# The further rounds of layer one: one guarded block at the last body instead of one at the head of each body

## What is computed

```python
def layer0(h, src, dst, w, W, b):
    h = h @ W + b
    msgs = w[:, None] * h[src]
    agg = segment_sum(msgs, dst, N)
    deg = segment_sum(w, dst, N)
    return relu(agg / (deg[:, None] + 1e-6))

def layer1(h, e, W_msg, b_msg, W_upd, b_upd, eps, src, dst):
    m = gelu(concatenate([h[src], e], -1) @ W_msg + b_msg)
    h = (1 + eps) * h + segment_sum(m, dst, N)
    return gelu(h @ W_upd + b_upd)

h = relu(layernorm(x));  x = x + layer0(h, src, dst, edge_weight, ...)
h = relu(layernorm(x));  x = x + layer1(h, edge_attr, ...)
```

## Time and profile before

| | us |
|---|---|
| runs | 2934.1, 2928.56, 2933.87 |
| median | 2933.87 |
| profiled execution, its time | 2940.75 |
| its span | 2938.9 |

### The profile page before, as it was taken

How to read it: one execution, slowest core, us unless ns; L and a number is a source line. 1 busy time by engine, 2 the same in 40 slices (tenths; PEclk the granted TensorE clock), 3 DMA queues, 4 the chain that set the end, 5 groups by cost and what they waited for, 6 DMA issues and landing times.

```text
span 2938.9 us, 72786 instructions
## 1 busy us (share of the span) xinstructions
PE 2615.2 (89%) x22325; PEld 2440.5 (83%) x22326; DVE 2088.3 (71%) x4375; ACT 1617.3 (55%) x5144; POOL 1820.8 (62%) x1911
## 2 busy tenths in 40 slices
PE   1788877887888888788999999999999999999999
PEld 1678777777777777777999999999999999999998
DVE  8766667667667666766777777777777777777774
ACT  2555555455555555545556656556656565665653
POOL 3355555555555555552777777777777777777771
PEclk9999998888888888888999999999999999999997
DMA  6010111110111111111454444544444545444442
GB/s 125 16 20 19 21 21 20 22 22 20 21 22 20 21 22 21 20 21 44 109 124 119 121 121 118 121 118 121 117 120 118 123 115 123 119 119 120 118 120 45
DMA packets 473383, 216.56 MB, mean 74 GB/s; under 512 B 264997, under 2 KB 442025, under 8 KB 473077
## 3 DMA queue, kind: packets, MB, share of 16 engines
q1 hardware_dynamic: 412404, 151.55, 19.8%
q0 software_dynamic: 60672, 62.25, 11.5%
HBM read 208.14 MB, written 5.51 MB: 73 GB/s over the span
## 4 chain that ended last, share of the span: by engine, by line
PE 52%; DVE 0%; ACT 0%; issue 0%; DVEq 0%
PE ps L917 38%; PE ps L1115 7%; PE ps L989 4%; PE ps L1104 3%; PE ps L1062 1%; PE ps L1018 0%; DVE rows L1446 0%; DVE parts L1211 0%; DVE sel L1442 0%; DVE room L1635 0%; ACT h_sb L847 0%; DVE h_sb L1666 0%; DVE h_sb L1671 0%; ACT h_sb L865 0%; DVE tick L1483 0%
## 5 line engine op out<-in xcount | busy, mean ns | idle before, releaser
L628 POOL DMA_INDIRECT rows<-p_table,idx x1176 | 1110.0, 944 | 395.5 <-issue 350.0
L917 PE MATMUL ps<-parts,pick_all 128*128 128x448 f32 x5488 | 1167.0, 369 | 2.2 <-DVE parts L1211 2.2
L917 PEld LDWEIGHTS ps<-parts,pick_all 128*128 128x128 f32 x5488 | 1017.8, 188 | 83.5 <-issue 2.6
L628 POOL DMA_INDIRECT rows<-h_table,idx x720 | 694.2, 964 | 616.1 <-ACT room L759 422.5
L720 ACT COPY adj<-ps 128x500 f32<-128x500 f32 (+1 forms) x848 | 394.8, 518 | 308.2 <-PE ps L927 298.0
L927 PE MATMUL ps<-hot_c,hot_p 128*128 128x125 f32 (+1 forms) x2336 | 470.7, 304 | 63.9 <-issue 57.3
L927 PEld LDWEIGHTS ps<-hot_c,hot_p 128*128 128x128 f32 x2336 | 393.0, 212 | 80.5 <-issue 72.2
L1442 DVE TENSOR_TENSOR sel<-ps,mask 128x896 f32<-128x896 f32 x196 | 214.0, 1092 | 310.1 <-PE ps L917 302.0
L1425 DVE TENSOR_SCALAR pick_all<-src_all,node_f 128x1792 fp32r<-128x1792 int16 x196 | 406.6, 2075 | 28.6 <-issue 26.2
L989 PE MATMUL ps<-onehot,room 128*65 128x72 f32 (+1 forms) x3400 | 227.0, 237 | 193.7 <-DVE onehot L1373 98.2
L989 PEld LDWEIGHTS ps<-onehot,room 128*65 128x65 f32 (+1 forms) x3400 | 197.7, 144 | 228.2 <-issue 118.2
(11 more groups left out here) (180 smaller groups left out, 2592.4 us busy)
## 6 DMA issues: line engine op xcount, KB each, us to landing
src_all<-keys SPq DMA_DIRECT2D x196, 448.0 KB
ea<-in_edge_attr_dram SPq DMA_DIRECT2D x196, 256.0 KB
rows<-p_table,idx POOLq DMA_INDIRECT x1176
rows<-h_table,idx POOLq DMA_INDIRECT x720
x_sb<-in_x_dram SPq DMA_DIRECT2D x6, 224.0 KB, 4.0
h_table<-h_sb SPq DMA_DIRECT2D x6, 224.0 KB
p_table<-h_sb SPq DMA_DIRECT2D x6, 224.0 KB
out_dram<-h_sb SPq DMA_DIRECT2D x6, 224.0 KB
```

The costliest lines, as they stand in the source:

```text
L628: nc.gpsimd.indirect_dma_start(out=rows[:, s, j, 0:D], out_offset=None, in_=table[:, :], in_offset=bass.IndirectOffsetOnAxis(ap=idx[:, s, ...
L917: last = nc.tensor.matmul(to, hot[:, k, t * P:(t + 1) * P], parts[:, part, k, :, :].rearrange("p a d -> p (a d)"), start=(k == 0 and part ...
```

## The change

`further_rounds` leaves the head of every body. A new function `all_rounds` is called in its place, but only in the last body of layer one (`if not ahead`), on PE and on DVE. It is guarded by one flag, `row_any`, the greatest of the bodies' bits, which one more reduction on DVE makes in the preparation. Inside it loops over the zones and their bodies with the old block. PE's wait on `s_sumTc` now stands before these loops and waits for all bodies' sums; an increment of `s_passed` next to it is gone.

```diff
@@ -256,6 +256,7 @@
         row_r = sb("row_r", [1, 3, BODIES])
         row_g = sb("row_g", [1, NG])
         row_b = sb("row_b", [1, BODIES, 2], i32)
+        row_any = sb("row_any", [1, 1], i32)
         slow_at = sb("slow_at", [1, SLOTS, JA], i32)
         node_i = sb("node_i", [P, 1], i32)
         with nc.sbuf_tensor("src_raw", [P, 2, G], i32) as src_raw, nc.sbuf_tensor("dst_raw", [P, 2, G], i32) as dst_raw:
@@ -959,13 +960,11 @@
                                             ones_col[:, :], start=True, stop=True)
                 last.then_inc(s_sum, 1)
 
-            def further_rounds(z, b, more):
-
-                with pe.If((more & (1 << SLOTS)) > 0):
+            def further_rounds(z, b):
+
+                with pe.If((more_flags(b) & (1 << SLOTS)) > 0):
                     count = pe.value_load(row_b[0:1, bass.ds(b, 1), 0], min_val=1, max_val=N)
                     before = pe.value_load(row_b[0:1, bass.ds(b, 1), 1], min_val=0, max_val=N * BODIES)
-                    pe.wait_ge(s_sumTc, b + 2)
-                    pe.sem_inc(s_passed, 1)
                     with pe.Fori(0, count) as i:
                         k = (before + i) * (TILES + 1)
                         for t in range(z.tiles):
@@ -1022,9 +1021,18 @@
                 blocks_of(ZONES[0], 0, s)
             adjacency_sums(ZONES[0], 0)
 
+            def all_rounds():
+
+                with pe.If(pe.value_load(row_any[0:1, 0:1], min_val=0, max_val=1) > 0):
+                    pe.wait_ge(s_sumTc, BODIES + 1)
+                    for z in ZONES:
+                        with pe.Fori(z.first, z.end) as b:
+                            further_rounds(z, b)
+
             def first(b, here, ahead, further):
                 more = more_flags(b)
-                further_rounds(here, b, more)
+                if not ahead:
+                    all_rounds()
                 if ahead:
                     blocks_of(ahead, b + 1, 0)
                 sums_back(here, b)
@@ -1314,6 +1322,7 @@
             meta(nc.vector.scalar_tensor_tensor(out=bits[:, :, 0], in0=row_r[:, 2, :], scalar=float(2 ** SLOTS),
                                                 in1=bits[:, :, 0], op0=ALU.mult, op1=ALU.add))
             meta(nc.vector.tensor_copy(row_i[:, :, 3], row_f[:, 2, :]))
+            meta(nc.vector.tensor_reduce(row_any[:, :], row_r[:, 2, :], AX.X, ALU.max))
             dve.wait_ge(s_base_ps, 1)
             meta(nc.vector.tensor_copy(base_bc[:, :], psS[:, 0:NG]))
             dve.wait_ge(s_dwt, 2)
@@ -1482,9 +1491,16 @@
 
                 nc.vector.memset(tick[:, s:s + 1], 0.0).then_inc(s_done, 1)
 
-            def further_rounds(z, b, more):
-
-                with dve.If((more & (1 << SLOTS)) > 0):
+            def all_rounds():
+
+                with dve.If(dve.value_load(row_any[0:1, 0:1], min_val=0, max_val=1) > 0):
+                    for z in ZONES:
+                        with dve.Fori(z.first, z.end) as b:
+                            further_rounds(z, b)
+
+            def further_rounds(z, b):
+
+                with dve.If((more_flags(b) & (1 << SLOTS)) > 0):
                     count = dve.value_load(row_b[0:1, bass.ds(b, 1), 0], min_val=1, max_val=N)
                     before = dve.value_load(row_b[0:1, bass.ds(b, 1), 1], min_val=0, max_val=N * BODIES)
                     with dve.Fori(0, count) as i:
```

## The result

| | before | after |
|---|---|---|
| median of the runs, us | 2931.22 (4 runs) | 2822.93 (4 runs, 2820.88 to 2834.17) |
| profiled execution, us | 2940.75 | 2820.88 |
| its span, us | 2938.9 | 2819.1 |
| granted clock of the span | 0.947 | 0.965 |

The ratio is 0.9639, with a 95% interval of 0.961 to 0.9667: 108 us faster in the median. The forecast was 2835, in a range of 2780 to 2873.

What follows compares the result with a forecast made beforehand. VectorE's serial stream with its hole was taken to bound layer one. Gains of 56.1 + 35.6 + 8 - 1 = 99 us took the profiled 2940.75 to 2842, and 7 less for the median gave 2835; range 2780 to 2873.

Steps and rivals of the forecast that it cites:

- The hole: VectorE's idle time in issue before each layer-one loop body, 7.5 to 8.2 us in zone 1, 6.8 in zone 0; code fetch.
- case (d): Rival: the hole is a fixed price of loads, compares and semaphores; gain only 5 to 10 us, about 2926; chance 0.05.
- The split of jump and back edge: Of VectorE's 7.6 us idle at a loop head, the jump over the rounds is about 3, the back edge about 4.
- The ring: VectorE's tile builds, TensorE's last window, sums and next tile product, whose release VectorE awaits: 25.45 us a body in zone 1.
- Case (a): Rival: the back edge keeps its stall; zone 1 stays at 25.45, zone 0 costs 4 us more, 2839; 0.72 together with the sum.
- zone 0's loop: Period falls from 21.97 to 19.0 us, the same kind of ring giving 18.8; 35.6 us over 12 bodies.
- zone 1's loop: Period falls from 27.32 to the ring's 25.45 us; 56.1 us over 30 bodies.
- the rest: Body 48's jump and flag load, 0.5 us, and one more VectorE reduction in the prologue, 0.3; together about -1 us.
- The straight bodies: Bodies outside the loops and the entries (14, 15, 16, 47): 2 us saved each, 8 in all, ends 0 and 10.
- Body 48: Keeps one jump, over about 530 VectorE instructions, with a second load of a flag; costs 0.5 us.
- case (b): Rival: fewer or shorter gaps give TensorE its full clock in the adjacency sums; 50 us more gain, 2785; chance 0.16.
- Case (c): Rival: TensorE's clock falls for the whole of the sums and tiles, sums about 14 us; about 2995; chance 0.02.

Runs made afterwards that it cites:

- e1b_dve_back: The changed kernel with VectorE's rounds put back at the head of every body, TensorE's at the last body only; 2925.06 us, ratio 0.9992.
- e2b_pe_back: The changed kernel with TensorE's rounds put back at the head of every body, VectorE's at the last body only; 2843.41 us, ratio 0.9715.
- e4_skip_a: The changed kernel with never-run blocks at VectorE's body heads: 40 instructions in zone 0's loop, 120 in zone 1's, 20 to 160 elsewhere; 2836.79 us, single run.
- e5_skip_b: The changed kernel with never-run blocks at VectorE's body heads: 100 instructions in zone 0's loop, 200 in zone 1's, 60 to 130 elsewhere; 2809.76 us, single run.
- e7b_hoist: The changed kernel with VectorE's one-hots of group 3 made ahead of four tile builds (zone 0: five) instead of behind them; 2671.63 us, ratio 0.9138.
- e11_before_hoist: The kernel before the change, with group 3's one-hots made ahead of four tile builds; 2918.96 us, ratio 0.9966.
- e8b_busy: The changed kernel with 28 products without use on TensorE in the gap before window 3 in zone 1; 2767.36 us, ratio 0.9452.

## Why the prediction was right, point by point

**The hole is fetched code, and DVE's.** Shown: e1b_dve_back brings hole, packets and time back; e2b_pe_back doesn't. In the body of the earlier trace rows four of its six packets stand inside the hole, between 925.1 and 932.7. A price of the instructions themselves, case (d), is out by the skips of 20 to 130.

**The split of jump and back edge** as about 3 and 4 us agrees in kind with the skip runs. There 3.7 to 4.0 us stand before a straight body with 240 skipped. A stalling back edge, as the loop bodies' idle time less that at the entry with the same jump, is 5.2 us in e4_skip_a and 2.7 in e5_skip_b, on either side of the 4. That a loop of 207 or 211 instructions has no stall at its back edge came out as hoped, at 1.2 us. My reason, that it is short, was too simple, as 334 and 350 show; that the changed kernel's loops don't stall was in part luck.

**The ring** was sized at 25.45 us and measured 25.61. By its links, from one wait of `hot_p` to the next, the body from 791.28 is 14.80 + 1.09 + 8.24 + 0.76 = 24.89, and the next, from 816.17, 14.88 + 1.40 + 9.22 + 0.78 = 26.28; the forecast had 14.84 + 1.06 + 8.81 + 0.74. The place, the order of its links and the wait that shows it (`hot_p` for PE, forecast up to 4.8 us a body, measured 142.2 us in 31) were right, and e7b_hoist and e11_before_hoist show it from both sides, e7b_hoist with the clock's share in it. The sums were taken at 8.65 us; they came out at 8.1 to 8.3 and 9.1 to 9.3 in turn, 8.67 in the mean. That the mean stayed, behind a longer gap, was in part luck. Case (a), that a stall of 4.5 us at the back edge wouldn't matter in zone 1, is borne out by e5_skip_b.

**What went where.** By the starts of PE's sums before and after, the gain of the profiled execution, 119.8 us of span where the forecast had 99, splits as follows:

| stretch | forecast | measured |
|---|---|---|
| zone 0's loop, with its first two bodies | 35.6 | 51.9 |
| bodies 14 and 15 and the entry of zone 1's loop, and body 47 | 8 | 13.7 |
| zone 1's loop | 56.1 | 52.6 |
| the rest | -1 | 1.7 |

**The term that was mis-sized is zone 0.** The rows gave a ring of 18.8 us, I took 19.0, and the kernel has 18.10. The link from the last window to the next product, 6.14 us in the earlier trace rows, held 0.69 us of issue on PE before its first tile. I carried it over whole. But PE's own jump was in it: with that jump back (e2b_pe_back) the period is 18.71, the ring of the rows, and without it 18.10. The prediction said of PE's jump that it counts in straight bodies and left it out in the loops. Together with the 19.0 taken for 18.8, this made 47.0 us in the 12 bodies for which 35.6 were forecast. The other part is the count: the first two bodies, which the rows didn't show, gave 4.9 us more.

**The straight bodies** were put at 2 us each, 8 in all, and gave 13.7, so 3.4 each, which is outside the 0 to 10 of the prediction. It kept 1.0 us of each gap for the flag's load. But PE's first tile, 2.3 to 3.9 us late with the jump in e2b_pe_back, had 0.02 us or nothing before it without.

**Body 48** was put at 0.5 us for its jump over about 530 instructions. DVE stands 4.70 us in issue there, against 3.48 before; no time was lost by it, as the row "the rest" shows.

**The clock**, case (b), didn't come by itself: PE's gap before window 3 grew from 2.22 to 3.27 us, as the prediction held against it, and the sums stayed slow. The size of the case, 50 us, is near what e8b_busy measured when the gap was filled (56 us). Case (c) didn't come: no sums took over 9.3 us. Why the low clock lasts longer in every other body stayed open.

## What to carry to other kernels

Idle time in "issue" at the head of a loop body, with packets on the instruction queue in each body, is code that is fetched again; move code that never runs out of the loop, and do it on the engine whose stream is serial. Before pricing such an edit, close the ring through the other engines: here DVE alone would, by the rows before, have gone to 20.6 us a body, and the ring stopped it at 25.6. Then ask which operation in that ring stands later than it need: one one-hot moved ahead of four builds gave 151 us, more than the change itself (of these, e8b_busy puts about 56 on TensorE's clock). In the kernel before, the same edit gave 8.

## What the runs showed of the hardware

- Skips on VectorE cost some tenths of a us up to 130 instructions, and 2 to 3 us more from 160 on, in straight code. In loops a skip of 140 in a loop of 350 cost 0.3 us (1.54 against 1.20), and one of 120 in a loop of 334 cost 5 us or more a body (6.3 to 7.1).
- The queue q14 moved packets of 8 KB, 5 or 6 in each body whose VectorE loop stalled and none in the others. Another, q8, moved 16 KB a packet and followed TensorE's code: 31 packets with its jump and 25 without, and none within its loops of 381 and 425 instructions.
- A gap of 3.27 us on TensorE was followed by sums of 8.1 to 9.3 us, of which 2.7 or 4.7 us at a granted clock of 0.50; with 2.47 us of the gap filled they took 6.98 at 1.00, and so did they (7.00) where the gap was gone.
- On one chip TensorE paused in the middle of runs of products, and the kernel before and four others took 3986 to 4030 us there.
